# Both operand transposes of x on VectorE, two operand tiles, GpSimd takes the low parts of P and Q

## The reference

```python
def xca(q, k, v):                                   # layer 0, in both directions (rgb = x, geo = y)
    attn = softmax(einsum('bhni,bhnj->bhij', q, k) * scale)
    return einsum('bhnd,bhde->bhne', v, attn)
rgb_att = rgb + xca(heads(rgb, wq_rgb), heads(geo, wk_point), heads(geo, wv_point)) @ proj_p2r.T
geo_att = geo + xca(heads(geo, wq_point), heads(rgb, wk_rgb), heads(rgb, wv_rgb)) @ proj_r2p.T
x1 = rgb_att + geo_att
# layer 1: q, k from y, v from x1
attn = softmax((Wq y + bq)(Wk y + bk)^T / sqrt(E))  # per head
o = Wo (attn (Wv x1 + bv)) + bo + x1
out = (o - mean(o)) * rsqrt(var(o) + EPS) * gn_w + gn_b   # mean and variance over channels and positions
```

## Time and profile before

| | us |
|---|---|
| median of 3 runs | 327.87 (327.06 to 328.1) |
| the profiled execution's own time | 328.15 |
| its span, first to last instruction | 326.3 |
| TensorE busy | 307.2 |
| VectorE busy | 261.7 |
| ScalarE busy | 233.1 |
| GpSimd busy | 190.1 |
| packets of the loads and stores | 73.87 MB, 226 GB/s over the span |

### The profile page before, as it was taken

One profiled execution on the slowest core, in us unless ns is written; L12 is line 12 of the kernel. 1 busy time (PEld: TensorE's weight loads), 2 busy tenths in 40 slices (PEclk: granted clock), 3 DMA queues, 4 the chain that ended last, 5 costly groups with the idle time before them and its releaser, 6 DMA issues.

```text
span 326.3 us, 12574 instructions
## 1 busy us (share of the span) xinstructions
PE 307.2 (94%) x4792; PEld 269.2 (82%) x4792; DVE 261.7 (80%) x707; ACT 233.1 (71%) x385; POOL 190.1 (58%) x277
## 2 busy tenths in 40 slices
PE   6999958999997899999999999999999999999990
PEld 4887857898986689898988989898988889898760
DVE  2495874988898498888889888888889898876883
ACT  2664734887878379787878779787878779787575
POOL 0874481675656647575766757575766746575611
PEclk9999999999999999999999999999999999999997
DMA  7999999179798985979899897979799895220036
GB/s 230 378 250 273 256 292 262 24 262 278 197 294 217 292 210 147 311 216 289 227 300 249 241 304 193 310 200 298 221 298 249 248 266 152 106 109 20 2 129 257
DMA packets 39060, 73.87 MB, mean 226 GB/s; under 512 B 4608, under 2 KB 26368, under 8 KB 39040
## 3 DMA queue, kind: packets, MB, share of 16 engines
q1 hardware_dynamic: 35008, 58.92, 66.7%
q10 hardware_dynamic: 4032, 14.68, 12.9%
HBM read 56.81 MB, written 16.78 MB: 226 GB/s over the span
## 4 chain that ended last, share of the span: by engine, by line
PE 91%; issue 3%; DVE 2%; DMA 1%; ACT 1%; SPq 0%; POOLq 0%; POOL 0%
PE oacc L427 10%; PE oacc L434 9%; PE oacc L428 8%; PE mid L530 4%; PE gacc L387 4%; PE mid L507 4%; PE mid L454 4%; PE stat L389 4%; PE tpx L344 4%; PE gacc L388 3%; PE gacc L389 3%; PE stat L387 3%; PE stat L388 3%; PE mid L516 2%; PE gacc L405 2%
## 5 line engine op out<-in xcount | busy, mean ns | idle before, releaser
L1135 POOL TENSOR_TENSOR xy_lo<-raw,xy_hi 128x256 fp32r<-128x256 f32 x256 | 179.5, 738 | 119.8 <-ACT xy_hi L704 119.8
L704 ACT ACTIVATE xy_hi<-raw 128x1024 fp32r<-128x1024 f32 x64 | 67.0, 1048 | 0.0
L866 DVE STREAM_TRANSPOSE t<-y_blocks 128x512 f32<-128x512 f32 x56 | 62.4, 1158 | 0.0
L711 ACT ACTIVATE res<-oacc 128x512 f32<-128x512 f32 x59 | 34.9, 593 | 29.0 <-PE oacc L434 28.7
L895 DVE BATCH_NORM_STATS2 hstat<-res 128x6 f32<-128x512 f32 x60 | 40.1, 687 | 15.5 <-ACT res L711 15.4
L427 PE MATMUL oacc<-xy_hi,pq_hi 128*128 128x512 f32 x120 | 52.4, 436 | 0.1
L428 PE MATMUL oacc<-xy_lo,pq_hi 128*128 128x512 f32 x120 | 47.4, 395 | 1.6 <-issue 1.6
L387 PE MATMUL gacc<-t 128*32 128x129 f32 x224 | 43.1, 273 | 2.6 <-issue 2.6
L390 PE MATMUL gacc<-t 128*32 128x225 f32 x224 | 45.4, 354 | 0.0
L389 PE MATMUL gacc<-t 128*32 128x225 f32 x224 | 45.4, 354 | 0.0
L390 PE MATMUL stat<-t 128*32 128x225 f32 x224 | 45.1, 353 | 0.0
(11 more groups left out here) (166 smaller groups left out, 905.3 us busy)
## 6 DMA issues: line engine op xcount, KB each, us to landing
raw<-in_x SPq DMA_DIRECT2D x31, 512.0 KB, 5.8
raw<-in_ctx SPq DMA_DIRECT2D x31, 512.0 KB, 6.9
y_blocks<-in_ctx SPq DMA_DIRECT2D x112, 128.0 KB, 7.0
out<-res ACTq DMA_DIRECT2D x28, 512.0 KB, 3.5
x_blocks<-in_x SPq DMA_DIRECT2D x56, 128.0 KB, 6.9
out<-res SPq DMA_DIRECT2D x4, 512.0 KB, 2.7
wt<-in_weights SPq DMA_DIRECT2D x1, 896.0 KB, 6.8
raw<-in_x SPq DMA_DIRECT2D x2, 256.0 KB, 3.8
```

The lines of the kernel that those rows point to most:

```text
L704: act.activation(xy_hi[slot][:, s, :], raw[slot][:, s, :], ACT.Copy).then_inc(split_hi, 1)
L866: dve.transpose(dst, blocks[:, HC * i:HC * (i + 1)]).then_inc(yt_ready, 1)
L1135: piece = pool.tensor_tensor(xy_lo[slot][:, s, cols], raw[slot][:, s, cols], xy_hi[slot][:, s, cols].bitcast(f32), ALU.subtract)
```

## The change

1. **Transposes of x.** From pair 2 on TensorE's `x_transpose` and ScalarE's `xt_out` are gone. VectorE transposes x of both tiles from `x_blocks`, which has four buffers in place of two; each pair loads 512 KB more. Tile 3 (pair 1) also comes in blocks, x and y, in place of early transposes by TensorE.
2. **Operand tiles.** `TB` is 2 in place of 4: tile b of every pair uses `t[b]`, so a transpose waits for the Gram of the same b of the pair before.
3. **Low parts.** ScalarE copies P and Q once more (`pq_copy`, into the new `pq_full`), and GpSimd subtracts `pq_hi` from the copy, one instruction for each tile.
4. **Bias of V.** The three `abv` instructions of `softmax_out` are gone; two matmuls of one column on `z` take the place of L521.
5. **Full-width Gram** in the pairs that are written out (now also pairs 2 and 3), the six-matmul form in the loop alone.
6. **Orders and banks.** The softmax tiles move from `mid` to `tpx`'s banks, which are free now. TensorE does part 0 of both halves of tile 0 before part 1. VectorE's transposes are spread over its step. ScalarE splits y of tile 0 later, and copies the Gram earlier. SyncE loads `x_blocks` of every tile; the weights have semaphores of their own.

```diff
-TB = 4
+TB = 2
             def refill_blocks(h, u, b):
                 sp.wait_ge(yt_ready, 2 * n + 2)
                 load_blocks(h + 1, 2 * u + b)
-                if b == 1:
-                    sp.wait_ge(xt_ready[1], n + 1)
-                    load_x_blocks(h + 1, u)
+                sp.wait_ge(xt_ready[b], n - b + 2)
+                load_x_blocks(h + 1, 2 * u + b)
...
-                pe.wait_ge(abv_ready, p + 1)
-                pe.matmul(mid0[:, 2 * C:2 * C + 2], w("oT"), abv[:, :], start=True, stop=True)\
-                    .then_inc(wo_abv_done, 1)
+                for a in range(2):
+                    mm = pe.matmul(mid0[:, 2 * C + a:2 * C + a + 1], z[:, a, 2, :], (col("bv"), col("bv", vec_rot))[a],
+                                   start=True, stop=True)
+                mm.then_inc(wo_bv_done, 1)
...
-                    gram_chunks(h, u, 0, 0, 4)
+                    chunks = gram_full_width if isinstance(p, int) else gram_chunks
+                    chunks(h, u, 0, 0, 4)
...
+            def pq_copy(p):
+                if not (isinstance(p, int) and p < 1):
+                    act.wait_ge(pqlo_ready, 2 * p)
+                act.activation(pq_full[:, :, :, :], mid1[:, :], ACT.Copy).then_inc(pq_copied, 1)
...
-            def pq_low(p, parity):
-                dve.wait_ge(pqhi_ready, p + 1)
-                dve.tensor_tensor(pq_lo[parity][:, :, :, :].rearrange("p a s c -> p (a s c)"), mid1[:, :],
...
+            def pq_low(p, parity):
+                pool.wait_ge(pqhi_ready, p + 1)
+                pool.wait_ge(pq_copied, p + 1)
+                for b in range(2):
+                    pool.tensor_tensor(pq_lo[parity][:, b, :, :], pq_full[:, b, :, :],
+                                       pq_hi[parity][:, b, :, :].bitcast(f32), ALU.subtract).then_inc(pqlo_ready, 1)
```

More of the change, by code:

```diff
@@ L76, in cross_attention_pair_kernel @@
         y_blocks = [sb(f"y_blocks{n}", [C, QUADS, N // QUADS]) for n in range(4)]
-        x_blocks = [sb(f"x_blocks{n}", [C, QUADS, N // QUADS]) for n in range(2)]
+        x_blocks = [sb(f"x_blocks{n}", [C, QUADS, N // QUADS]) for n in range(4)]
         xy_hi = [sb(f"xy_hi{n}", [C, 2, N], f32r) for n in range(4)]
@@ L332, in _ @@
             pe.wait_ge(ones_set, TB)
[L334 to L345, removed]
             def x_transpose_early(n, i):
@@ L430, in out_half @@
                     return
-                if half == 0 and b == 0:
-                    pe.wait_ge(pqlo_ready, 2 * h + u + 1)
+                if half == 0:
+                    pe.wait_ge(pqlo_ready, 2 * (2 * h + u) + b + 1)
                 for s in range(2):
@@ L830, in _, with prepare_mask, prepare_weights @@
             dve.wait_ge(attn_zero, 2 * QUADS)
-            def prepare():
+            def prepare_mask():
+                s1 = float(C) ** -0.5
                 dve.wait_ge(consts_in, 16)
-                dve.wait_ge(weights_in, 80)
+                dve.wait_ge(small_in, 32)
+                dve.tensor_scalar(nbq[:, :], col("bq"), s1 * N, None, ALU.mult).then_inc(mask_ready, 1)
+                dve.tensor_copy(mask6[:, 0:4, :], other_head.unsqueeze(1).broadcast_to([C, 4, W32]))
+                dve.wait_ge(mask_ready, 1)
+                for a in range(2):
+                    last = dve.scalar_tensor_tensor(out=mask6[:, 4 + a, :], in0=bk32, scalar=nbq[:, :],
+                                                    in1=other_head, op0=ALU.mult, op1=ALU.add)
+                last.then_inc(mask_ready, 1)
+            def prepare_weights():
+                dve.wait_ge(weights_in, 16)
                 s0, s1 = float(C // H) ** -0.5, float(C) ** -0.5
@@ L1030, in step @@
                 if front and not middle:
-                    for b in range(2):
-                        for i in range(2):
-                            y_early_out(b, i)
-                    prepare()
+                    y_early_out(0, 0)
+                    y_early_out(0, 1)
+                    prepare_mask()
+                    y_early_out(1, 0)
+                    y_early_out(1, 1)
+                    prepare_weights()
                     gram_mirror(p)
@@ L1074, in step @@
                     c_out(p - 1, 1 - u)
+                    if ahead:
+                        y_transpose(h + u, 1 - u, 0, 1)
                 elif middle:
                     half_stats(*before(h, u), 1, 1)
[L1077 removed]
+                    u3_out(p - 1)
                     half_moments(p - 3)
[L1079 to L1081 removed]
+                    shift_scores(p - 1)
+                    softmax_out(p - 1)
                     partition_moments(p - 3, 1 - u)
```

271 lines of the change are left out of this document (128 added, 143 removed).

## The result

The changed kernel takes 331.6 us (median of 5 runs, 330.28 to 345.27), the kernel before 327.87 beside it; ratio 1.0162, 95% interval 1.0108 to 1.0215. It is slower, where 318.0 was forecast. The profiled execution took 334.0 us with a span of 332.2, 5.9 longer than that of before.

A forecast was written before the change was run, and what follows sets the result against it. TensorE was taken to bound the kernel before, at 18.33 us a pair. From 328.15: loop -7.0, pairs 2 and 3 -4.8, first pass +1.9, start -0.3, tail +0.3, sum -9.9, 318.2 (median 318.0); range 312 to 324.5.

The forecast's parts named there:

- Loads, "I take 0": All pairs: 0.52 MB more a pair, 19.9 us of packet time, by 1.15 is 17.3, under 17.75; no cost.
- The 15 us of lead: In the loop, y blocks were taken to land some 15 us ahead of use, x blocks 19 us.
- the loads are the bound: Rival, chance 0.12: in the loop packets don't overlap, VectorE waits for blocks; 19.9 us a pair, 11 more, 329.
- First pass, +1.9 with 0 to 3.7: Pairs 4 and 5: existing gaps stay, one more of mean size is added, +1.9 us, between 0 and 3.7.
- The loop, 17.75: 12 loop pairs: 17.75 us each in place of 18.33, between 17.5 and 18.1; 7.0 us saved.
- the 17.3 to 17.5 forecast: In the loop, a sign: VectorE busy some 17.3 to 17.5 us a pair, with waits under 0.5 in all.
- Pairs 2 and 3, -4.8: Written-out pairs 2 and 3: issue gaps go with the full-width Gram, -4.5, other work -0.3; -4.8 us together.
- Start, -0.3: Start of the kernel: tile 3's early transposes go (1.7 us of TensorE); -0.3 us, between 0 and -1.5.
- Tail, +0.3, bounds 0 to 1: Tail: low parts by copy and GpSimd +0.5, bias matmuls less the abv chain -0.2; +0.3 us, bounds 0 and 1.

The follow-up runs named there:

- the run with the blocks' order: The changed kernel with the four loads of a block tile issued in the order 0, 2, 1, 3; 326.76 us, ratio to before 1.0001.
- the run held twice: The changed kernel, loads in order 0, 2, 1, 3, SyncE holding loads back in the loop's first and second pass (until pair 5's first-tile Gram); 322.27 us.
- full-width alone: The kernel before with only the full-width Gram in pairs 2 and 3, its loop unchanged; 322.73 us, ratio 0.9876.
- both simple parts: The kernel before with the full-width Gram in pairs 2 and 3 and blocks loaded in the order 0, 2, 1, 3; 322.58 us, ratio 0.9884.
- the light loads: The changed kernel with tile 0's x_blocks loads cut to 16 elements a partition in the loop; 328.37 us, ratio to before 1.0086.
- the loads alone: The kernel before, also loading 512 KB of x more a pair into a tile nobody reads; 338.25 us, ratio 1.0344.
- loads held back: The changed kernel, blocks in order 0, 2, 1, 3, with pair 7's second-tile loads issued only after pair 4's Gram; 324.68 us, ratio 0.9953.

## Why the prediction was wrong, point by point

**Loads, "I take 0": the first step that failed.** The packet time of 19.9 us a pair was near the truth: in the loop of the changed kernel the same blocks of two pairs landed 20.1 us apart (mean of six pairs), where TensorE took 17.94. Then I divided by 1.15 because a share over 1 says that packets overlap. But 1.15 came from a stretch of 1 KB pieces in which each packet was slowed by the others (226 GB/s; a 1 KB packet took 82 ns there and 72 in the loop of before), so the overlap was paid for in the packets' own length. In the loop the share stood at 1.07 to 1.08 and the rate at 266 to 269 GB/s. The 15 us of lead failed too. I took them from the loop of before, where blocks land 17 to 24 us ahead of their transposes. In the changed kernel the dense loads ahead of the loop had left almost nothing of it:

| x blocks of | landed, us | first transposed, us | lead | lead with the order 0, 2, 1, 3 |
|---|---|---|---|---|
| pair 5, tile 0 | 83.5 | 86.0 | 2.5 | 11.6 |
| pair 6, tile 1 | 109.6 | 123.2 | 13.6 | 22.4 |
| pair 9, tile 1 | 169.6 | 177.0 | 7.4 | 17.9 |
| pair 12, tile 1 | 230.5 | 230.9 | 0.4 | 17.9 |
| pair 13, tile 1 | 250.7 | 250.7 | 0.0, after a wait of 1.20 | 18.2 |

The lead grew while TensorE stood and ran slowly in the first pass, and from 123 us on 2.2 us of it went with every pair. Cost: pairs 12 to 15 took 78.89 us where in the run with the blocks' order they take 73.04: 5.85, which is also what VectorE's seven waits for blocks add up to (5.89). The rival "the loads are the bound" had the mechanism, at a chance of 0.12; its formula with the measured numbers, 12 x (19.6 - 17.94) - 15, gives 4.9, but that it comes so near is luck, since neither the 12 pairs nor the 15 us are what the trace shows. The two losses also depend on each other: with a lead of 2.5 us at 86, a first pass without its 9.9 us would have brought the waits earlier.

**First pass, +1.9 with 0 to 3.7: the second.** Pairs 4 and 5 took 45.82 in place of 2 x 17.94, 9.9 too much, where before had 40.57 - 2 x 18.35 = 3.9. So 6.0 were added, outside the bounds. The cause was named rightly (code beside dense DMA), but priced by gaps of before of 1.55 to 2.61. The gaps are 5.66 here; most of the rest is the clock behind them. The windows of the changed kernel behind its first gap (the granted clock is the third number from the right):

```profile
82.00:86.00 4.00, 1.88 (x45) 1.45 (x38) 3.83 (x9) 3.05 (x4) 1.17 (x3) 0.88 1.10 227
86.00:88.00 2.00, 2.00 (x39) 1.89 (x30) 1.06 (x2) 0.00 (x0) 2.00 (x4) 0.50 1.02 387
88.00:90.00 2.00, 2.00 (x36) 1.43 (x31) 0.95 (x4) 1.06 (x2) 0.51 (x1) 0.89 1.04 405
```

TensorE did 1.88 us of work in four, and then was granted 0.50, which is the level of 1.2 GHz. This lasted from 85.0 to 88.4 us, and it came again from 112.3 to 115.7: 6.8 us at half the clock, some 3.4 lost, an estimate that leaves 0.9 of the 9.9 open. In before the gaps were followed by 1.00 over the loop's first pass (mean of 60 to 120 us; here 0.94), and so was the gap of 2.90 in the run held twice; what decides it isn't shown. I had read the rule of the Trainium skill (Runtime: NRT & Kernel Launch, Instruction fetch mechanics), that crossing into a new block of code is mostly hidden, as one that would take my 1.9 away. The runs show both: hidden with DMA at 0.34, and at 1.07 where the full-width form stood in the loop, but not at 1.08 with the six-matmul form.

**The loop, 17.75.** It is 17.94, within the bounds of 17.5 to 18.1. TensorE's terms: transposes -0.88 as said; the bias is 0.34 (L511) in place of 0.12, +0.22 and not +0.12; `pq_products` 1.16 in every pair, +0.27, since it waits for nmat; Gram +0.04. 18.33 - 0.35 = 17.98. I had this sum as 17.8 and then went 0.05 under it. Over 11 pairs -4.3 in place of -7.0 over 12: the last step of the loop, 19.2, gained nothing. VectorE came to 17.3, in the 17.3 to 17.5 forecast, and never waited for the Gram: the two operand tiles cost nothing to be seen. Four operand tiles beside four `x_blocks` weren't tried.

**Pairs 2 and 3, -4.8.** Measured -3.9. Pair 2 gave -4.4 with its gaps gone, as said. Pair 3 cost 0.5 more than before (18.71 against 18.19), where I had -0.1. The size of the full-width form was off: it takes 3.73 us for the first tile and 3.48 for the second (L396 in the run with that form everywhere), 7.21 a pair against 6.38 (159.76 to 166.14 in the chain of the changed kernel), so +0.83 and not +0.62; less the 0.39 of the new order this is 0.44, most of what pair 3 shows.

**Start, -0.3.** It reads +1.4, but the start differs by more than that from one execution to the next. Kernels with the start of before reached `pq_products` at 33.35, 35.08 (full-width alone) and 35.14 us (both simple parts); the changed kernel and those made from it did so at 33.41 to 34.91. So this term can't be told from 0, in spite of a new gap of 1.10 at 27.93, and that before's profile began at 33.35 was luck.

**Tail, +0.3, bounds 0 to 1.** It was +1.0, 0.5 in each of the two last steps, where I had +0.5 once and -0.2 for the bias. The copy is on the chain in both, GpSimd's low part, as said, in the last one. In the run with the blocks' order, whose tail is the changed kernel's with another execution's times:

```profile
297.23 0.59 ACT pq_full L677
...
308.08 0.60 ACT pq_full L677
...
308.81 0.74 POOL pq_lo L1136
```

**The sum.** +1.4 - 3.9 + 6.0 + 5.7 - 4.3 + 1.0 = +5.9 (5.7 is the loads' part of the last four intervals against the profile of before). Forecast was -9.9. Of the 15.8 us between, 5.7 are the loads, 4.1 the first pass, 2.7 the loop, 1.7 the start, 0.9 pairs 2 and 3, and 0.7 the tail. Six tenths are the two terms that hang on the 512 KB more a pair, on a DMA that was at 0.91 to 0.97; that all of the first pass's 4.1 comes from them is argued, not measured, since the light loads left its gaps.

## What to carry to other kernels

When DMA is over 0.9 of a loop, don't divide packet time by a share over 1: take the packet time as it is for a pass, as an upper price (19.9 us here, 20.1 measured in the changed kernel, but the loads alone got by in 18.37); follow the lead of the loads from the start of the kernel and not from its steady loop, and see how much of it goes with each pass. Price a transfer that nobody waits for by what else uses the engines: here 512 KB a pair of unread data cost 11 us, through gaps at code that was met for the first time and the slower clock behind them. And before trading bytes for engine time, try the part that only removes code: by itself it gave as much as any version here.

## What the hardware showed that I had not expected

- A transfer of code (16 KB, 0.9 to 1.5 us of packet time) can come late when DMA is dense: in the first pass it was moved at 82.2 us in the changed kernel and at 78.5 with loads held back. Gaps of TensorE of 1.1 to 5.8 us stand where new code is met for the first time and nowhere later: 7.5 us in before, 13.4 with 10% more bytes, none in the loop where the six-matmul form was gone from the code, and none at a place where DMA stood at 0.34; over the four us ahead of each gap its share was 0.91 to 1.12. Dense loads alone don't make a gap (1.07, and none, with the full-width form in the loop). The page counts 13 such transfers before, 10 with the full-width form written out, 8 with it everywhere.
- The order in which four loads of 32 partitions each are issued changes DMA's rate: 251 against 274 GB/s ahead of the loop at the same share of 1.09, with the same packets. In the loop of the changed kernel it was 266 to 269 in the order 0, 1, 2, 3 and 282 to 290 in the order 0, 2, 1, 3; but 284 was reached in the first order too, with the loads alone.
- The share doesn't tell a backlog, landing time does. A load of 512 KB took 14.0 us to land in the changed kernel (share 1.07 to 1.08 in the loop), 5.9 with the loads alone (0.99 to 1.07), and 5.0 with the other order (0.99 to 1.01).
